# Gate and up by seven block products instead of eight, with saved weight combinations and a second phase for the down projection

## What is computed

```python
conv = conv1d(x, weight, padding=4, groups=4)      # 8 channels per group, 9 taps
h    = conv + (cond @ c_weight.T)[:, :, None] + bias[None, :, None]
ht   = h.reshape(-1, 512)                          # 4096 rows
up   = ht @ W_up.T                                 # 1376 x 512 weights
gate = silu(ht @ W_gate.T)
out  = x + ((gate * up) @ W_down.T).reshape(x.shape)
```

## Time and profile before

| | |
|---|---|
| median of three runs | 831.0 us |
| lowest and highest | 830.52 and 832.48 us |
| profiled execution: span from first to last instruction | 829.1 us |
| busy in it: TensorE, VectorE, ScalarE, GpSimd | 98%, 35%, 22%, 5% |
| granted TensorE clock, mean | 0.998 |
| moved by DMA | 42.75 MB, mean 52 GB/s |

### The profile page before, as it was taken

One profiled execution on the slowest core, in us unless ns is written; L12 is line 12 of the kernel. 1 busy time (PEld: TensorE's weight loads), 2 busy tenths in 40 slices (PEclk: granted clock), 3 DMA queues, 4 the chain that ended last, 5 costly groups with the idle time before them and its releaser, 6 DMA issues.

```text
span 829.1 us, 9744 instructions
## 1 busy us (share of the span) xinstructions
PE 813.3 (98%) x3715; PEld 660.8 (80%) x3715; DVE 294.0 (35%) x466; ACT 183.8 (22%) x314; POOL 45.1 (5%) x68
## 2 busy tenths in 40 slices
PE   5989999999999999999999999999999999999998
PEld 4778887888878888788887888788887888878886
DVE  3733444433333222533334222343333322242223
ACT  4821433111121111311112111211112111121111
POOL 2200110101000000011100000010100000000000
PEclk9999999999999999999999999999999999999999
DMA  7252220311113000121112200031111200011001
GB/s 228 72 154 86 78 54 26 126 51 52 26 25 127 1 1 0 53 77 51 51 26 75 78 0 1 1 128 51 51 26 26 101 1 1 0 58 45 1 0 51
DMA packets 54059, 42.75 MB, mean 52 GB/s; under 512 B 5024, under 2 KB 43072, under 8 KB 54016
## 3 DMA queue, kind: packets, MB, share of 16 engines
q1 hardware_dynamic: 54016, 42.12, 17.0%
HBM read 25.32 MB, written 8.39 MB: 41 GB/s over the span
## 4 chain that ended last, share of the span: by engine, by line
PE 95%; DVE 1%; DMA 1%; SPq 1%; ACT 1%; issue 0%; ACTq 0%; DVEq 0%
PE up_ps L552 29%; PE acc L568 29%; PE gate_ps L552 29%; PE conv_ps L516 2%; PE conv_ps L509 2%; PE xt_ps L485 2%; DMA bias_col<-in_fside_S 1%; ACT perm_early L638 1%; SPq L313 0%; DMA down_nat<-in_L_ffn_W_down 0%; DVE xt_lo L755 0%; PE xt_ps L535 0%; DVE res L867 0%; PE conv_ps L535 0%; SPq L350 0%
## 5 line engine op out<-in xcount | busy, mean ns | idle before, releaser
L847 DVE TENSOR_TENSOR act_f<-gate_ps,act_f 128x512 f32<-128x512 f32 (+1 forms) x88 | 60.8, 691 | 339.5 <-ACT act_f L680 339.5
L552 PE MATMUL up_ps<-h_hi,wgu_hi 128*128 128x512 f32 (+1 forms) x352 | 141.9, 403 | 0.0
L552 PE MATMUL up_ps<-h_hi,wgu_lo 128*128 128x512 f32 (+1 forms) x352 | 139.2, 395 | 0.0
L552 PE MATMUL up_ps<-h_lo,wgu_hi 128*128 128x512 f32 (+1 forms) x352 | 139.0, 395 | 0.0
L568 PE MATMUL acc<-wd_hi,g_hi 128*128 128x512 f32 (+1 forms) x352 | 138.8, 394 | 0.0
L552 PE MATMUL gate_ps<-h_lo,wgu_hi 128*128 128x512 f32 (+1 forms) x352 | 137.8, 392 | 0.0
L552 PE MATMUL gate_ps<-h_hi,wgu_hi 128*128 128x512 f32 (+1 forms) x352 | 137.8, 391 | 0.0
L568 PE MATMUL acc<-wd_hi,g_lo 128*128 128x512 f32 (+1 forms) x352 | 137.6, 391 | 0.0
L552 PE MATMUL gate_ps<-h_hi,wgu_lo 128*128 128x512 f32 (+1 forms) x352 | 137.4, 390 | 0.0
L568 PE MATMUL acc<-wd_lo,g_hi 128*128 128x512 f32 (+1 forms) x352 | 137.1, 389 | 0.0
L680 ACT ACTIVATE act_f<-gate_ps 128x512 f32<-128x512 f32 (+1 forms) x88 | 52.6, 598 | 377.7 <-PE gate_ps L552 376.9
(11 more groups left out here) (116 smaller groups left out, 520.0 us busy)
## 6 DMA issues: line engine op xcount, KB each, us to landing
res<-in_x SPq DMA_DIRECT2D x32, 256.0 KB, 3.4
out_y<-res SPq DMA_DIRECT2D x32, 256.0 KB, 2.2
x_in<-in_x SPq DMA_DIRECT2D x13, 512.0 KB, 3.8
stage<-win SPq DMA_DIRECT2D x104, 64.0 KB, 2.0
down_nat<-in_L_ffn_W_down SPq DMA_DIRECT2D x10, 256.0 KB, 3.2
w_early<-in_L_ffn_W_gate SPq DMA_DIRECT2D x6, 256.0 KB, 7.1
w_early<-in_L_ffn_W_up SPq DMA_DIRECT2D x6, 256.0 KB, 7.0
x_first<-in_x SPq DMA_DIRECT2D x3, 512.0 KB, 8.2
```

Of the source, the lines that this page charges most:

```text
L552: mm = pe.matmul(bank[0:w, :], wt[:, i, which, f * P:f * P + w], hv[:, i, :], start=i == 0 and n == 0, stop=i == KC - 1 and n == 2)
L847: dve.tensor_tensor(act_f[0:w, :], gate_ps[0:w, :], act_f[0:w, :], ALU.mult).then_inc(silu_done, 1)
```

## The change

**Block products.** The gate and up weights of a hidden chunk form a 2 x 2 block matrix: rows gate and up, columns the two halves of D (2 chunks each). The activations of a group form another: the two halves of D by the two blocks, a and b, of 512 tokens. Eight block products of 2 chunks x 3 terms = 6 matmuls gave gate and up for both blocks. Now there are seven (kinds 0 to 6), in Winograd's form of Strassen's scheme. Four of them take combinations of weights (T1 = up1 - gate1, T2 = up2 - T1, T3 = T2 - gate1, T4 = gate2 - T2; kinds 3, 2, 4, 5) and four combinations of activations (S1 = b1 + b2, S2 = S1 - a1, S3 = a1 - b1, S4 = a2 - S2). Every operand is split into high and low parts as before.

**Additions.** Kinds 0, 2, 4 and 5 of a chunk accumulate in one bank, and ScalarE copies its contents out after 0, 2 and 4 (`copy_chain`); the next of them waits for that copy. Kind 1 goes to `second_ps`, 3 and later 6 to `third_ps`. VectorE makes the gate of a (kind 1 + copy 0), the up of b (third + copy 4, before kind 6 is added), the up of a (third + copy 2); the gate of b is the chain's bank itself. Per chunk and group that is three copies and two sigmoids on ScalarE and seven full-size operations on VectorE.

**Two phases.** The gated products of a group stay in `g_all` (float32, all 11 chunks, both blocks). When the first phase (77 products) is done, the second multiplies them with the down weights: 22 units of 12 matmuls, split just ahead. The first unit stands between products 4 and 5 of the last chunk. The order of units is block a then b in group 0, and alternating in the others. Residuals are loaded into `stage` (and, for the first block, into `mix`, which holds the copies).

**Weights.** The high and low parts of a weight combination fill a slot of 256 KB in a ring of 14. In group 0 they are made (per chunk: one full and seven half-size operations on ScalarE, seven half-size ones on VectorE, two permutations with wraps and four half-size subtractions on GpSimd) and stored to a DRAM tensor `saved`; in groups 1 to 3, and for block b's down units of group 0, they are loaded again, 14 slots ahead. Only the first chunk's gate and up and the transposes of the second are prepared before the first product. The four activation combinations are made by VectorE in group 0 (by chunk) and by GpSimd for the others (`mix_h`, 1024 columns each), and split within the second phase, one kind per down unit (units 11 to 18 in group 0, 2 to 9 in groups 1 and 2). The loops over groups are unrolled. SyncE now stages both blocks' channels of a chunk together.

The diff, cut (lines of the new kernel; on VectorE the order of a chunk stands last):

```diff
+    phase1 = [(0, 0)]
+    for f in range(FC):
+        phase1 += [(f, k) for k in (1, 2, 3, 4)] + ([(f + 1, 0)] if f + 1 < FC else []) + [(f, 5), (f, 6)]
+    place = {fk: n for n, fk in enumerate(phase1)}
+    PRODUCTS = len(phase1)
+    SAVED = PRODUCTS + 2 * FC
+    FIRST = PRODUCTS + 4 * FC
+    UNITS = 2 * FC
+    NS = 14
...
+        saved = nc.dram_tensor("saved", [SAVED, P, TOK], F32, kind="Internal").ap()
...
+            def save_products(f):
+                for kind in (0, 1, 6, 3, 2, 4, 5):
+                    sp.wait_ge(w_made[kind], f + 1)
+                    save_slot(product_at(0, f, kind))
...
+            def refill(s):
+                new = s + NS
+                if new >= TOTAL or is_made(new):
+                    return
+                used, count = last_use(s)
+                sp.wait_ge(used, count)
+                if is_made(s):
+                    sp.wait_ge(slot_stored[s % NS], LD * made_in_slot(s))
+                if group_of(new) < 2:
+                    first = saved_index(new)
+                    sp.wait_ge(slot_stored[first % NS], LD * made_in_slot(first))
+                sp.dma_start(ring[:, new % NS, :].bitcast(F32), saved[saved_index(new)]).then_inc(slot_loaded[new % NS], LD)
...
+            load_x(0, 1)
+            load_nat(0)
+            load_x(0, 2)
+            load_nat(1)
+            load_x(0, 3)
+            stage_chunk(0, 0)
+            load_nat(2)
+            stage_chunk(0, 1)
+            save_products(0)
+            sp.wait_ge(x_blocked, 2)
+            load_x(1, 0)
+            stage_chunk(0, 2)
+            stage_chunk(0, 3)
+            load_nat(3)
...
+                    save_down(0)
+                    sp.wait_ge(g_done[0], FC)
+                    sp.wait_ge(g_done[1], FC)
+                    load_res(0, 0)
+                if g + 2 < G:
+                    sp.wait_ge(x_blocked, STEPS * (g + 2))
+                    load_x(g + 2, 0)
...
+                for m, (f, half) in enumerate(units(g)):
+                    if g == 0 and half == 0 and f + NDOWN < FC:
+                        load_down(f + NDOWN)
+                    if g == 0 and half == 0 and f + 1 < FC:
+                        save_down(f + 1)
+                    if g == 0 or half == 1:
+                        for part in range(2):
+                            refill(down_at(g, f, half, part))
...
+            def mix_h(g):
+                pool.wait_ge(hc_done[RAW_B2], hc_count(g))
+                for half in range(2):
+                    for i in range(KC):
+                        pool.wait_ge(staged[half][i], LD * OB * (g + 1))
+                a1, a2, b1, b2 = stage[:, 0, 0:2, :], stage[:, 0, 2:4, :], stage[:, 1, 0:2, :], stage[:, 1, 2:4, :]
+                pool.tensor_tensor(b2, b1, b2, ALU.add).then_inc(s_done[K_S1], 1)
+                pool.wait_ge(s_done[K_S1], hc_count(g))
+                pool.tensor_tensor(b1, a1, b1, ALU.subtract).then_inc(s_done[K_S3], 1)
+                pool.wait_ge(s_done[K_S3], hc_count(g))
+                pool.wait_ge(hc_done[RAW_A1], hc_count(g))
+                pool.tensor_tensor(a1, b2, a1, ALU.subtract).then_inc(s_done[K_S2], 1)
+                pool.wait_ge(s_done[K_S2], hc_count(g))
+                pool.wait_ge(hc_done[RAW_A2], hc_count(g))
+                pool.tensor_tensor(a2, a2, a1, ALU.subtract).then_inc(s_done[K_S4], 1)
...
+            def product(g, f, kind):
+                n, w, s = FC * g + f, width(f), product_at(g, f, kind)
+                bank = (chain_ps[f % 2], second_ps, chain_ps[f % 2], third_ps, chain_ps[f % 2], chain_ps[f % 2], third_ps)[kind]
+                if g == 0:
+                    pe.wait_ge(w_made[kind], f + 1)
+                else:
+                    pe.wait_ge(slot_loaded[s % NS], LD * loads_in_slot(s))
+                if kind == 0:
+                    if f > 1:
+                        pe.wait_ge(silu_b_done, n - 1)
+                    elif g > 0:
+                        pe.wait_ge(y_added, 2 * OB * (g - 1) + OB + f + 1)
+                    elif f == 1:
+                        pe.wait_ge(toep_done, 1)
+                elif kind == 1:
+                    if f > 0:
+                        pe.wait_ge(gate_a_done, n)
+                    elif g > 0:
+                        pe.wait_ge(y_added, 2 * OB * (g - 1) + OB + 3)
+                    else:
+                        pe.wait_ge(toep_done, 1)
+                elif kind == 2:
+                    pe.wait_ge(copied0, n + 1)
+                elif kind == 3:
+                    if f > 0:
+                        pe.wait_ge(up_a_done, n)
+                    elif g > 0:
+                        pe.wait_ge(y_added, 2 * OB * g)
+                    else:
+                        pe.wait_ge(conv_out, CPG)
+                elif kind == 4:
+                    pe.wait_ge(copied2, n + 1)
+                elif kind == 5:
+                    pe.wait_ge(copied4, n + 1)
+                else:
+                    pe.wait_ge(up_b_done, n + 1)
+                fresh = kind in (0, 1, 3)
+                for q in range(2):
+                    if f == 0:
+                        pe.wait_ge(hc_done[kind], hc_count(g, q))
+                    for t, (wt, hv) in enumerate(terms(slot_w(s, 0, q, w), slot_w(s, 1, q, w), hc_hi[:, kind, q, :], hc_lo[:, kind, q, :])):
+                        mm = pe.matmul(bank[0:w, :], wt, hv, start=fresh and q == 0 and t == 0, stop=q == 1 and t == 2,
+                                       skip_group_check=not fresh)
+                mm.then_inc(product_done[kind], 1)
...
+                elif f == 0:
+                    pe.wait_ge(g_done[0], FC * (g + 1))
+                    pe.wait_ge(silu_b_done, FC * (g + 1))
...
+                product(g, 0, 0)
+                for f in range(FC):
+                    product(g, f, 1)
+                    if conv and f < STEPS:
+                        turn_x(g + 1, f)
+                    if g == 0 and f == FC - 1:
+                        turn_down(0)
+                    product(g, f, 2)
+                    product(g, f, 3)
+                    if conv and f == 1:
+                        conv_head(g + 1)
+                    if conv and 1 <= f <= STEPS:
+                        conv_step(g + 1, f - 1)
+                    product(g, f, 4)
+                    if g == 0 and f + 2 < FC:
+                        turn_gate(f + 2)
+                    if f + 1 < FC:
+                        product(g, f + 1, 0)
+                    else:
+                        if g == 0:
+                            turn_down(1)
+                        down(g, 0)
+                    product(g, f, 5)
+                    if g == 0 and f + 2 < FC:
+                        turn_up(f + 2)
+                    product(g, f, 6)
+                for m in range(1, UNITS):
+                    if g == 0 and m + 1 < FC:
+                        turn_down(m + 1)
+                    down(g, m)
...
+            def prepare(f, part):
+                w = width(f)
+                if part == 0:
+                    act.wait_ge(gate_turned, f + 1)
+                    if f > 0:
+                        act.wait_ge(t_done[T1], f)
+                        act.wait_ge(t_done[T4], f)
+                    hi(x_gate[:, :, 0:w], gate_ps[:].rearrange("p (i f) -> p i f", i=KC)[:, :, 0:w]).then_inc(gate_kept, 1)
+                    act.wait_ge(gate_kept, f + 1)
+                    w_raw(f, RAW_A1, x_gate[:, 0:2, 0:w])
+                    w_raw(f, RAW_A2, x_gate[:, 2:4, 0:w])
+                elif part == 1:
+                    act.wait_ge(up_turned, f + 1)
+                    w_raw(f, K_S4, up_ps[:].rearrange("p (i f) -> p i f", i=KC)[:, 2:4, 0:w])
+                elif part == 2:
+                    w_mixed(f, K_S1)
+                    w_mixed(f, K_S2)
+                else:
+                    w_mixed(f, K_S3)
+                    w_mixed(f, RAW_B2)
...
+            def copy_chain(n, f, kind):
+                done, to, copied = {0: (product_done[0], copy0, copied0), 2: (product_done[2], copy2, copied2),
+                                    4: (product_done[4], copy4, copied4)}[kind]
+                act.wait_ge(done, n + 1)
+                if n > 0 and kind == 0:
+                    act.wait_ge(gate_a_done, n)
+                elif n > 0 and kind == 2:
+                    act.wait_ge(g_done[0], n)
+                elif n > 0:
+                    act.wait_ge(g_done[1], n)
+                w = width(f)
+                hi(to[0:w], chain_ps[f % 2][0:w, :]).then_inc(copied, 1)
...
+            def gate_a(n, f):
+                dve.wait_ge(product_done[1], n + 1)
+                dve.wait_ge(copied0, n + 1)
+                if n > 0:
+                    dve.wait_ge(g_done[0], n)
+                w = width(f)
+                dve.tensor_tensor(act_a[0:w], second_ps[0:w, :], copy0[0:w], ALU.add).then_inc(gate_a_done, 1)
...
+                    silu_a(n, f)
...
+                    up_b(n, f)
```

(4 more changed lines are left out.)

1049 lines of the change are left out of this document (584 added, 465 removed).

## The result

| | before | after |
|---|---|---|
| median, us (ten runs each, same chip) | 830.24 | 833.0 |
| lowest and highest | 828.62, 832.48 | 830.43, 835.86 |
| profiled execution: span | 829.1 | 828.8 |
| mean granted clock in it | 0.998 | 0.967 |

The ratio is 1.0034, 95% interval 1.0017 to 1.005. The kernel is slower by a third of a per cent, where 813 was forecast. Of the experiments' runs one execution, in run 1, was slow (1960.94 us); that run's ratio leaves it out, its median of four does not.

A forecast was written before the change was run, and what follows sets the result against it. TensorE, busy 813 of 829.1 us, was taken as the bound. Start, TensorE work and tail 781.7, clock 1.6, boundary waits 13.8 and group 0's down-weight waits 14.1 made 811.2 us of span; with 1.9 for the median, 813 us, range 799 to 831.

The forecast's parts named there:

- the three boundaries: Phase boundaries of groups 1 to 3: TensorE waits 3.0 us for VectorE at each, 4.6 with the clock, 13.8 in all.
- The clock's price of 1.6: TensorE's clock halves after a wait of 2 us or more, losing 1.6 us each time.
- (a): Rival: inside steps, ScalarE's copy of product 2 or 4 comes late; 0.8 us per step gives 848; chance 0.09.
- (d): Rival: reloading weight slots in groups 1 to 3 is too slow; about 853 us at 180 GB/s; chance 0.02.
- the slack: Between product 2 and product 4, which waits for ScalarE's copy of 2: 0.4 us to spare, the least anywhere.
- So the convolution ends at about 40 us, as now: Start: earlier staging copies offset new VectorE and ScalarE work between convolution steps, at 0.4 us per half-tile operation.
- Then the queue of SyncE decides: Start: SyncE's staging, loads and saves set the pace after the convolution; the last staged data land at 50 us.
- the forecast's 55.8: Start of the third product, in us, after staging, splits and ScalarE's copy of the first product; bounds 50 and 60.
- what costs nothing while its cover lasts: Inside steps: other engines' work hides behind TensorE's; in group 0, ScalarE 7.0 and VectorE 9.0 us in 12.
- I take the middle, 9.5: Group 0's phase boundary: TensorE's wait in us for the third block of down weights, between 8.2 and 10.9.
- Rival (b): Extra GpSimd load is dear: 7.5 us at group ends, half a microsecond per group 0 step; 826 us, chance 0.17.
- the full-size rows, all near 0.69, do not show it: Profile rows of full-size VectorE operations, at 0.69 us, taken as evidence against slowing of two-SBUF-input operations beside GpSimd.

The follow-up runs named there:

- run 11: Kernel after, with ScalarE's copy of product 2 made twice in groups 1 to 3: 841.02 us, ratio 1.0136.
- run 1: Kernel after, with the down weights needed first in group 0's second phase loaded before the residuals, later blocks one unit earlier: 821.81 us, ratio 0.9863.
- run 5: Kernel after, with GpSimd bringing the first two half chunks of x into blocks before permuting the first weights: 828.2 us, ratio 0.9981.
- run 7: Kernel after, with VectorE subtracting the low parts of two raw gate halves from the PSUM bank instead of ScalarE's SBUF copy: 832.37 us, ratio 1.0039.
- run 9: Kernel after with six edits (run 1, run 3, run 4, run 5 among them), run 7's, and group 1's x ahead of staging chunks 2 and 3: 791.47 us.
- Run 3: Kernel after, with the next convolution's head multiplied at the end of step 0 and read early in step 1: 827.42 us, ratio 0.9965.
- run 4: Kernel after, with the four activation combinations for the next group made by VectorE instead of GpSimd: 826.14 us, ratio 0.9959.
- best2: The kernel of run 10, that is run 9 with later residual and group 2 x loads and an earlier first copy: 780.96 us, ratio 0.9417.
- run 10: Against run 9: residuals and group 2's x loaded at down unit 8, first product copied before ScalarE's second half of the splits: 780.96 us, ratio 0.9417.

## Why the prediction was wrong

Three terms of the sum failed: the end of the convolution, a stall in the first phase of group 0 that it put at nothing, and the size of the wait for down weights. They are taken in turn, after what held.

**What held.** The removal: 264 matmuls at 0.23. A product cost 1.36 (forecast 1.379; in group 3, for one, two products lie 2.72 apart). Groups 1 to 3 and the tail came to 546.0 for 548.1, less 1.1 and 1.0. Each of the three boundaries shows a distance of 2.98 between matmuls, a wait of 2.75, for the 3.0 forecast. The clock's price of 1.6 held in after where it was paid, behind two of the three boundaries and not behind the third. Rivals (a) and (d) were rightly small: in after no step waits for a copy or a reloaded slot, and run 11 puts the slack at 0.33. The queue moved 151.72 MB without a wait of TensorE on `ring`.

**The start (+6.8).** The step that failed is "So the convolution ends at about 40 us, as now". It charged the new work between convolution steps by its own length alone, 0.4 us an operation, and never laid out GpSimd's order: `permute(0)` stands ahead of the blocks of x, and TensorE needed one of them at once. That was a wait of 7.7 us. The convolution ended at 50.7, and at 43.5 with that order mended (run 5: first product 6.6 earlier). VectorE's part was mis-sized too, 2.54 us for two operations taken as 0.8, but what that cost at the end of the chain is not shown (run 7). The 4 us that were still missing to 40 in run 9 are not divided. The next sentence, "Then the queue of SyncE decides", failed as well. The rest of the chain, from the end of the convolution to the third product, took 62.6 − 50.7 = 11.9, against 15.8; the forecast let SyncE's saves stand before the staging, and by 50.7 they had long been issued (38.5 to 42.5). The last staging round followed the end of the convolution in after, and also where the convolution came early: it ended at 43.5 in run 5 and at 44.1 in run 9, and the round was issued to the end 5.0 and 5.1 later. Had the convolution ended at 40 the queue would have counted (in run 5 it was through with chunk 2 at 42.9), but no run got there. So the 55.9 of run 9 beside the forecast's 55.8 is luck: a convolution 4.1 us later, and a chain behind it 4.1 shorter.

**Group 0, first phase (+6.4).** This stall stood nowhere in the sum. Under "what costs nothing while its cover lasts", VectorE's load in a step of group 0 was added up (9.0 us in 12) and taken as covered, without asking what VectorE does *before* the one read that TensorE needs within the same step. In step 1, `read_head` is queued behind the weights, and TensorE waits 3.8 us, then runs at half clock. Run 3 gave back 4.9. Of the rest, 1.0 is a wait for down weights at 188.5, and 0.3 the half clock behind the start, nine matmuls at 0.43 for the 1.6 put; the remaining 0.2 is spread.

**Group 0, second phase (+6.5).** The step "I take the middle, 9.5": the cause was foreseen and its size too small. TensorE stood 11.2 us for the load, beyond the upper end of 10.9. The later down loads cost 2.3, 1.9 and 0.4 us, 4.6 for the 3 put, and the clock 2.0 for 1.6. Another 1.5 is lost at 264.0, where VectorE's split stood beside GpSimd's `mix_h`, and 0.5 before the first product of group 1; some 0.7 is spread. Run 1 confirms the cause: the loads' place in SyncE's program. Residuals that nothing needed before the end of the phase stood in front of weights that were needed at once.

**Rival (b), with 0.17, was the nearest one,** and right in kind: GpSimd's load was dear. It was wrong in the way. The combinations took 2.40 where VectorE left them alone and up to 3.25 beside it, for the 2.25 put, and TensorE never waited for them; the cost is VectorE standing still beside them, 1.2 to 1.5 us per group (run 4: span −3.3). The step that failed is the sentence "the full-size rows, all near 0.69, do not show it". The row with 691, `act_f<-gate_ps,act_f`, reads PSUM with one input, so it could not show it. Of the full-size operations with both inputs in SBUF, `g_lo` is one, and its longest in the kernel before was no 0.69:

```profile
L755 DVE TENSOR_TENSOR g_lo<-act_f,g_hi x88: 679/692/981, 53.1 to 821.7; 128x512 fp32r<-128x512 f32 x80, 96x512 fp32r<-96x512 f32 x8
```

The six of 88 that ran beside a GpSimd copy took 0.77 to 0.98 (the 0.98 at 187.32, the copy from 186.63 to 187.76); the mean of 0.70 hid them. Where GpSimd is at work more, a pair of such operations took 2.54 us against 0.76 (run 7). The rule that the prediction cited from the Trainium skill, "GPSIMD Engine Reference", section "Key points", that GpSimd contends with instructions of VectorE that have two SBUF inputs, was the better guide; these traces agree with it.

The range ended at 831, and 833.0 lies outside. Its upper end was rival (b) and the start's bound, 60; what happened was a part of (b) and three misses of 6.4 to 6.8 us, each in group 0, where four engines' programs had been rewritten and only SyncE's had been followed row by row.

**What is not settled.** Why the half clock follows one wait of 2.6 us and not another was not tried. Starts of different executions were compared by one trace each. In best2 TensorE still waits 4.8 us for the last chunk of staged data and 3.2 in the convolution; whether those can go too was not tried. Of the edit of run 7 alone no gain in time is shown, and in run 9 it came together with another; the two of run 10 were not separated either.

## What to carry to other kernels

When a change removes work from the engine that sets the time, the gain is real, but it is paid out only if every queue is followed through the first iteration, where new work is made; a schedule that was even becomes one with edges. Write out for each engine what stands ahead of the one operation that the bottleneck needs, above all loads that nobody wants yet: here some ten edits, most of them moves of a few lines, made a change worth 5.8% out of one worth nothing (ratio 0.9417 against 1.0034). A sum of busy times that fits into a step shows nothing about the order within it, and an expected wait below 0.3 us must be looked for in the distances between matmuls and in the weight loads, not in the list of waits.
